# Removing 37 filler matmuls at nine places near the end of a four-layer decoder kernel

## What is computed

```
x = _layernorm(x + _L3_attn_ref(x, w_qkv, w_out, ...))      # 32 heads of 32
x = _layernorm(x + _L3_xattn_ref(x, ctx_1024, ctx_1024, mask_BxS2_bf1, ...))   # 16 heads of 8
x = _layernorm(x + _L3_ffn_ref(x, weight, gamma, beta))     # quantized by the maximum over all of x

# _L3_xattn_ref
scores = jnp.einsum('bnlh,bnph->bnlp', qm, km) / np.sqrt(HEAD_DIM)
attn = jax.nn.softmax(jnp.where(mask, scores, MASK_FILL), axis=-1)
out = jnp.einsum('bnlp,bnph->bnlh', attn, vm)
return out @ Wo.T + bo
```

## Time and profile before

| | us |
|---|---|
| median of three executions | 1298.23 |
| those executions | 1296.92 to 1298.74 |
| the profiled execution, its own time | 1299.21 |
| its span, first to last instruction | 1297.5 |
| PE busy | 1159.9 (89%) |
| DVE busy | 910.8 (70%) |
| ACT busy | 688.2 (53%) |
| POOL busy | 234.1 (18%) |
| mean granted clock of TensorE | 0.963 |

### The profile page before, as it was taken

The page is one execution under the profiler, slowest core; times in us unless marked ns, Lnnn a source line. Parts: engine busy times, 40 slices in busy tenths (PEclk is TensorE's granted clock), DMA queues, the critical chain, the costliest instruction groups (busy, mean ns, idle before and its releaser), DMA issues. The chain is left out here.

```text
span 1297.5 us, 27470 instructions
## 1 busy us (share of the span) xinstructions
PE 1159.9 (89%) x10601; PEld 788.4 (61%) x10601; DVE 910.8 (70%) x2412; ACT 688.2 (53%) x1307; POOL 234.1 (18%) x335
## 2 busy tenths in 40 slices
PE   7789999999999999999889899797768898799975
PEld 4457767777777777676556575465445565456542
DVE  5472573646689859988888689957785866756376
ACT  2254464544564655455657546575426755377534
POOL 4320131203110120022201023011120112301122
PEclk8899999999999999999999999999969999899997
DMA  7002101111112101110000000000000000000000
GB/s 289 20 2 65 50 17 48 35 58 42 50 34 74 50 25 50 34 49 1 2 9 10 2 26 1 1 2 1 2 1 2 2 2 3 1 2 2 2 1 33
DMA packets 23288, 35.59 MB, mean 27 GB/s; under 512 B 4584, under 2 KB 12920, under 8 KB 22904
## 3 DMA queue, kind: packets, MB, share of 16 engines
q1 hardware_dynamic: 23160, 33.83, 8.3%
HBM read 32.77 MB, written 1.05 MB: 26 GB/s over the span
## 5 line engine op out<-in xcount | busy, mean ns | idle before, releaser
L2252 DVE TENSOR_REDUCE arena<-banks 128x4 f32<-128x1024 f32 x128 | 150.5, 1217 | 69.4 <-PE banks L2078 68.7
L1366 PEld LDWEIGHTS banks<-WE,arena 128*128 128x128 f32 x1536 | 180.2, 192 | 24.5 <-issue 23.6
L1366 PE MATMUL banks<-WE,arena 128*128 128x128 f32 x1536 | 182.6, 276 | 0.0
L1410 ACT ACTIVATE arena<-banks,BC 128x512 f32<-128x512 f32 x192 | 128.3, 691 | 94.3 <-PE banks L1350 94.1
L1350 PE MATMUL banks<-XT,WE 128*128 128x512 f32 x384 | 177.3, 597 | 0.5 <-ACT arena L1842 0.3
L2232 ACT ACTIVATE arena<-banks 128x1024 f32<-128x1024 f32 x128 | 124.1, 1022 | 63.2 <-PE banks L2103 63.2
L1450 DVE SCALAR_TENSOR_TENSOR R<-banks,arena,R 128x128 f32<-128x128 f32 x256 | 71.8, 343 | 103.2 <-PE banks L1366 102.6
L2333 POOL TENSOR_TENSOR arena<-arena 128x256 f32<-128x256 f32 x56 | 43.4, 774 | 379.8 <-ACT arena L2214 379.8
L615 ACT COPY arena<-banks 128x512 f32<-128x512 f32 x100 | 57.1, 587 | 99.7 <-PE banks L610 40.4
L1350 PEld LDWEIGHTS banks<-XT,WE 128*128 128x128 f32 x384 | 68.2, 190 | 65.7 <-issue 62.8
L1912 DVE TENSOR_TENSOR arena<-arena 128x512 f32<-128x512 f32 x144 | 100.8, 700 | 4.0
(11 more groups left out here) (333 smaller groups left out, 2117.0 us busy)
## 6 DMA issues: line engine op xcount, KB each, us to landing
WE<-in_weights SPq DMA_DIRECT2D x64, 256.0 KB, 2.9
WE<-in_weights SPq DMA_DIRECT2D x64, 128.0 KB, 2.2
WS<-in_weights SPq DMA_DIRECT2D x1, 2368.0 KB, 14.5
RW<-in_rows SPq DMA_DIRECT2D x1, 1032.0 KB
XALL<-in_x SPq DMA_DIRECT2D x4, 256.0 KB, 10.9
out_dram<-arena SPq DMA_DIRECT2D x4, 256.0 KB, 2.3
WS<-in_weights SPq DMA_DIRECT2D x1, 900.0 KB, 9.2
WS<-in_weights SPq DMA_DIRECT2D x1, 645.0 KB, 9.3
```

The lines of the kernel that those rows point to most:

```text
L1366: ins = PE.matmul(v[:, tile(t)], self.HT[:, e % 2, j, tile(t)], self.W[:, (8 * i + e) % RING, 1, j], start=j == 0, stop=j == self.J - 1)
L1410: A.activation(self.HT[:, e % 2, j], psum.view(f"{self.L}.h{i}.{e}.{j}"), ACT.Relu, bias=bcol(self.p + "_b1", e * self.J + j))\
L2252: V.tensor_reduce(big.mx[:, 2 * pair:2 * pair + 2], v, AX.X, ALU.max, negate=True).then_inc(dve.read(f"big.m{i}.{n}.{pair}"), 1)
```

## The change

Nine entries of `FILLERS` are taken out: `big.o3.15` (2), `x3.pv2.1` (6), `x3.o.out2` (3), `x3.hT3.0` (6), `x3.hT3.1` (4), `x3.pv3.1` (6), `x3.pn3.1` (3), `x3.oT3` (4) and `x3.o.out3` (3). The numbers add up to 37 (the change's own title says 36). A name that is not in the table gets no filler. Nothing else differs.

```
-    "x2.xT3": 7, "big.xT2": 12, "lora.zT3": 5, "lora.xT3": 12, "big.hT3.0": 3, "big.o3.15": 2, "x3.pv2.1": 6,
-    "x3.o.out2": 3, "big.xT3": 27, "x3.hT3.0": 6, "x3.hT3.1": 4, "x3.pv3.1": 6, "x3.pn3.1": 3, "x3.oT3": 4,
-    "x3.o.out3": 3, "last.max": 22,
+    "x2.xT3": 7, "big.xT2": 12, "lora.zT3": 5, "lora.xT3": 12, "big.hT3.0": 3,
+    "big.xT3": 27,
+    "last.max": 22,
```

## The result

| | before | changed |
|---|---|---|
| median, us | 1298.22 | 1300.72 |
| lowest to highest, us | 1294.42 to 1301.46 | 1296.06 to 1305.08 |
| executions | 22 | 22 |
| the profiled execution, its own time, us | 1299.21 | 1302.22 |
| its span, us | 1297.5 | 1300.0 |

The ratio of changed to before is 1.0024, with a 95% interval from 1.0013 to 1.0035. The medians are 2.5 us (0.19%) apart, so the slowdown lies right at the edge of 0.2%. So it is slower, by 2.5 to 4 us.

The account below looks back on a forecast made before the run. A relay between PE, ACT, DVE and POOL was taken to bound the kernel. Clock fall 1.9 less own time 0.3 gave 1.6 us, of which 1.3 was kept on the 1298.23 median: 1299.5 us, range 1297.3 to 1301.8.

Parts of the forecast that it names:

- A: The forecast itself: one clock dip over the last x3's two scores, 1299.5 us (1298.2 to 1300.8); chance 0.61.
- The fillers' own time: Nine places: of the 37 fillers' 8.3 us of PE, only 0.3 us comes back, at big.o3.15 and x3.pv3.1.
- A fall before the scores: Last x3: without fillers PE is too sparse from 1253.5, so the clock falls where it showed 1.00 before.
- The comparison of the earlier trace with 973 to 977: There PE was busy 2.27 of 4.00 us and the clock fell; the stretch from 1253.5 would be emptier.
- rival B: Last x3: the clock holds, or as often as before, so only 0.3 us counts: 1297.9 us; chance 0.21.
- Its price: Both sequences' scores at half clock in the last x3, each 1.20 us becoming 2.16: 1.9 us more.
- The clock back before the second probabilities: Last x3: second scores and first probabilities run back to back without a wait, so the clock returns before the second probabilities.
- rival C: Clock stays low from the last x3 until the last.max fillers: 1302.7 us, up to 1306.5; chance 0.13.
- A fifth taken off: Some executions of before already lose the clock in the last x3, so 0.8 x 1.6 = 1.3 us is kept.
- D: The chain's reading is right and L506's 5.5 us come off the path: 1292.7 us; chance 0.03.
- E: The table changes nothing, as a name is not looked up or a number lives elsewhere: 1298.2 us; chance 0.02.
- within 0.2%: Whole kernel: the time differs from before by at most 0.2%, 2.6 us; chance 0.80.

Follow-up runs that it names:

- the second sample: The changed kernel again with only a comment added, timed later beside the experiments: ratio 1.0032 to the kernel before (1.0016 to 1.0048).
- no_shift_fillers: Kernel before with only the ten fillers of x3.hT3.0 (six) and x3.hT3.1 (four) taken out: ratio 1.0025 to before (1.0011 to 1.0038).
- no_late_fillers: Kernel before with only the sixteen fillers of x3.pv3.1, x3.pn3.1, x3.oT3 and x3.o.out3 taken out: ratio 1.0023 to before (1.0007 to 1.0039).
- one_less_at_last: Kernel before with one of the 22 fillers at last.max taken out, in idle time: ratio 0.9996 to before (0.9977 to 1.0015).
- no_early_fillers: Kernel before with only the eleven fillers of big.o3.15, x3.pv2.1 and x3.o.out2 taken out: ratio 1.0024 to before (1.0010 to 1.0039).
- after_maxima_fillers: Changed kernel with 13 fillers added ahead of the last Cross attention's two maxima (seven and six): ratio 1.0029 to before (1.0013 to 1.0046).

## Why the prediction was right, and where it was off

Forecast was 1299.5 us, 1.3 above the median, and 1300.72 came out, 2.5 above, inside the range from 1297.3 to 1301.8. The mechanism was A with a second fall that no rival had. The place in the range is partly luck: the sum of the forecast was 1.6 us where the traces show 3.0 (3.05 less the 0.07 of the early places), and the second sample, 4.1 us above the executions of before beside it (1302.96 and 1298.84), would have lain outside. Of the 1.4 us that were missing, 0.75 is the second fall, 0.4 to 0.5 own time and releases, 0.2 the price of the first.

- **The fillers' own time: 0.3 us back.** Mis-sized. The early places give back 0.07 us, and the steps behind the second scores lose 0.20. One error was the release. I allowed 0.06 us from an operand to its product, from rows in which fillers had just run. Behind a bare wait it is 0.14: the copy ends at 1269.42 + 0.59 = 1270.01 and L1095 starts at 1270.15, and the exponentials end at 1265.45 + 2.12 = 1267.57 with L1084 at 1267.72, 0.15. So each place that ended in a tie before now pays about 0.08. The other was `big.o3.15`: its values start 0.25 us behind their exponentials without the fillers, 0.30 with them, so 0.05 came back there and not 0.2; why a release takes that long at this place stays open. Own time is slightly against the change, by 0.1 us.
- **A fall before the scores.** Right in place and kind. The comparison of the earlier trace rows with 973 to 977 held: the clock fell although the longest bare wait ahead of it is 1.61 us in the rows above. That stretch was not the nearest of its kind, though: the clock also fell at about 1113.4, after 1.36 us of work in the 3.4 from 1110, for 7 us. The Trainium skill, page "TensorE: Matmul & The Clock Gate", table in "Why this matters for your kernels", names only long idle gaps. By that rule rival B would have come; the trace does not agree, with 1.61 us as its longest wait.
- **Its price: 2 x 0.96 = 1.9 us.** 2.25 and 2.25 against 1.20 are 2 x 1.05 = 2.1. The factor is 1.9 where I had 1.8. Start of the first scores to start of L600: 14.5 forecast, 15.02 measured.
- **The clock back before the second probabilities.** Right: L1084 at 1267.72 takes its 1.07. What I left out is that it is lost again. Behind the second probabilities the bare waits of 0.77, 1.00 and 0.77 us come close together, and L600 ran at half clock, 0.75 us more. This is the step that failed: I priced a return as final, and any loss of clock behind it at nothing. The sixteen late fillers held that second fall off: with them in place L600 took 1.16 us in no_shift_fillers, and without them alone 2.05 in no_late_fillers. Whether transposes hold the clock less than other matmuls, as rival C had it, no run here separates.
- **A fifth taken off** for executions of before that lose the clock anyway. Such executions exist (0.8 to 0.9 us each, two of five traces), so the deduction was in order, and 0.4 of 0.85 is 0.3 us, as much as was taken off. Two in five traces is a rough share. 3.1 us in the last stretch less 0.3 is 2.8, where 2.5 and later 4.1 were measured.
- **C** had L600 at half clock, but through a fall that lasts, and that did not come. Its argument from the earlier trace rows was weak: the slice that reads 6 holds two falls of 10.2 and 13.6 us, so not every dip was short.
- **B, D, E** fell. D most clearly: with 5.5 us of L506 off the chain's list the kernel got slower, since the chain had put waits down to the fillers that stood in them.
- **The chances.** 0.80 on "within 0.2%" was too sure: the ratio sits at the edge, and the second sample is beyond it. My A took one dip; A and a second dip should have had the larger share of what I gave C.

## What to carry to other kernels

Count a filler, or any busywork, twice: by the wait that it stands in, where its own time is mostly nothing while the clock is full, and by the real matmuls behind it whose clock it holds up. Before taking such work out, look at the stretch as it will be without it, and compare it with a stretch of the same trace after which the clock was lost; and go on past the return of the clock, because the next sparse stretch can lose it again. And where executions differ by 2 us, judge a 1 us edit by the distance between two instructions around it, in traces of both kernels, and use copies of the kernel to learn what the medians are worth.

## What was not expected

- A matmul behind a bare wait starts 0.14 us after its operand, one that comes after fillers 0.06 us (four places of the last Cross attention; the values of head group 15 take 0.25).
- Fillers at half clock can be the path: in no_late_fillers 22 of them took 6.72 us, and L2397 started 0.73 us after its operand; in no_shift_fillers and one_less_at_last six of them cost 0.45 and 0.57 us.
- The clock over the first scores was not tied to the six fillers next to them: in one trace 13 fillers ahead of the maxima held it, over scores that start 3.3 us behind the last of them.
- At 100 us from the start, where all these kernels have the same instructions, profiled executions were up to 5.1 us apart (no_early_fillers 4.0 behind before, after_maxima_fillers 1.2 ahead), which is more than the whole effect.
